# Two gated layers with a routed expert stage: expert outputs stored in blocks and gathered per token, 28 experts' weights kept

## The reference, cut to what matters

```
x = x + tanh(g_xattn[0]) * _L0_xattn_ref(ctx_512, _layernorm(x, axis=-1), ...)
x = x + tanh(g_ffn[0]) * _L0_ffn_ref(_layernorm(x, axis=-1), ...)
x = x + tanh(g_xattn[1]) * _L1_xattn_ref(...)
x = x + tanh(g_ffn[1]) * _L1_ffn_ref(_layernorm(x, axis=-1), ...)

def _L1_ffn_ref(hidden_states, gate_w, w_gate, w_up, w_down):
    probs = jax.nn.softmax(router_logits.astype(jnp.float32), axis=-1)
    top_vals, top_idx = jax.lax.top_k(probs, TOP_K)          # 8 of 64 experts for each of the 1024 tokens
    top_vals = top_vals / jnp.sum(top_vals, axis=-1, keepdims=True)
    rw = rw.at[jnp.arange(T)[:, None], top_idx].set(top_vals)
    g = jnp.einsum('th,ehi->tei', x, w_gate)                 # 256 -> 96
    u = jnp.einsum('th,ehi->tei', x, w_up)
    h = jax.nn.silu(g) * u
    h = h * rw[:, :, None]
    out = jnp.einsum('tei,eih->th', h, w_down)               # 96 -> 256
```

## Time and profile before

| | us |
|---|---|
| median of 3 runs | 408.3 |
| lowest and highest | 407.87, 409.57 |
| the profiled execution, its own time | 411.4 |
| its span, first to last instruction | 409.7 |
| PE busy in the span | 289.1 (71%) |
| DVE busy | 231.8 (57%) |
| POOL busy | 212.3 (52%) |
| ACT busy | 138.5 (34%) |
| moved by DMA | 98.39 MB, 240 GB/s over the span |

### The profile page before, as it was taken

How to read it: one execution, slowest core, us unless ns; L and a number is a source line. 1 busy time by engine, 2 the same in 40 slices (tenths; PEclk the granted TensorE clock), 3 DMA queues, 4 the chain that set the end, 5 groups by cost and what they waited for, 6 DMA issues and landing times.

```text
span 409.7 us, 7438 instructions
## 1 busy us (share of the span) xinstructions
PE 289.1 (71%) x2042; PEld 234.1 (57%) x2042; DVE 231.8 (57%) x1114; ACT 138.5 (34%) x393; POOL 212.3 (52%) x257
## 2 busy tenths in 40 slices
PE   5898168127810610899876778989899977871997
PEld 1345057126810510788765666878788855541886
DVE  0799999989397472355632433565655533331352
ACT  2263354315634420244432233444444432320000
POOL 2632013013358777777777777777777774540000
PEclk9999999657975555799999899999999999975899
DMA  4899997270016633999999999749999999726991
GB/s 134 306 341 300 302 322 226 80 228 3 1 48 224 232 128 131 316 330 324 324 331 311 338 326 318 234 136 297 301 326 300 305 289 267 214 58 251 346 299 62
DMA packets 72983, 98.39 MB, mean 240 GB/s; under 512 B 13007, under 2 KB 66144, under 8 KB 71920
## 3 DMA queue, kind: packets, MB, share of 16 engines
q1 hardware_dynamic: 63728, 79.03, 63.0%
q0 software_dynamic: 9216, 18.90, 14.5%
HBM read 62.23 MB, written 39.85 MB: 249 GB/s over the span
## 4 chain that ended last, share of the span: by engine, by line
PE 44%; DVE 22%; DMA 14%; POOL 9%; issue 5%; SPq 3%; ACT 3%; DVEq 0%; POOLq 0%; ACTq 0%
PE psum L756 16%; PE psum L765 10%; POOL expert_rows L514 8%; PE psum L812 7%; DVE work L1036 5%; DMA token_picks<-down_w,target 5%; DVE top L1032 5%; PE psum L745 4%; DMA gu_w<-expert_rows 3%; DMA sim<-expert_rows 3%; DVE xn L1154 2%; DVE stats L1007 2%; PE psum L576 2%; PE psum L570 2%; DMA sim<-token_picks 1%
## 5 line engine op out<-in xcount | busy, mean ns | idle before, releaser
L765 PE MATMUL psum<-proj_t,gu_w 96*96 96x256 f32 x254 | 77.5, 387 | 5.0 <-DVE gu_w L1247 5.0
L514 POOL DMA_INDIRECT expert_rows<-x_rows,place_at x64 | 62.5, 977 | 23.8 <-issue 22.9
L534 POOL DMA_INDIRECT token_picks<-down_w,target x64 | 58.7, 917 | 25.1 <-issue 14.4
L534 POOL DMA_INDIRECT token_picks<-adj,target x63 | 57.8, 917 | 22.5 <-issue 13.7
L967 ACT ACTIVATE gu_w<-psum 96x96 f32<-96x96 f32 x127 | 31.3, 246 | 108.2 <-PE psum L756 107.7
L1247 DVE TENSOR_TENSOR gu_w<-gu_w,psum 96x96 f32<-96x96 f32 x127 | 31.6, 249 | 56.8 <-ACT gu_w L967 56.0
L756 PE MATMUL psum<-gu_w,wgu 128*96 128x96 f32 x504 | 56.0, 256 | 7.7 <-DVE gu_w L1242 7.6
L756 PEld LDWEIGHTS psum<-gu_w,wgu 128*96 128x96 f32 x504 | 49.8, 170 | 9.6 <-DVE gu_w L1242 9.3
L1242 DVE COPY gu_w<-psum 128x192 f32<-128x192 f32 x127 | 43.7, 344 | 0.0
L745 PEld LDWEIGHTS psum<-ident,gu_w 96*128 96x128 f32 x160 | 22.0, 145 | 30.0 <-issue 12.3
L745 PE MATMUL psum<-ident,gu_w 96*128 96x96 f32 x160 | 27.7, 256 | 15.0 <-DMA gu_w<-expert_rows 14.4
(11 more groups left out here) (182 smaller groups left out, 448.2 us busy)
## 6 DMA issues: line engine op xcount, KB each, us to landing
expert_rows<-empty_rows SPq DMA_DIRECT2D x1, 15360.0 KB, 69.8
wgu<-in_L_ffn_w_gate_up SPq DMA_DIRECT2D x57, 192.0 KB
proj_t<-in_L_ffn_w_down SPq DMA_DIRECT2D x113, 96.0 KB
gu_w<-expert_rows SPq DMA_DIRECT2D x80, 120.0 KB
base<-in_L_ffn_w_gate_up SPq DMA_DIRECT2D x35, 192.0 KB
sim<-expert_rows SPq DMA_DIRECT2D x48, 120.0 KB, 2.0
pen<-in_L_ffn_w_gate_up SPq DMA_DIRECT2D x21, 192.0 KB
gu_w<-in_L_ffn_gate_up_proj SPq DMA_DIRECT2D x4, 512.0 KB, 8.1
```

Source lines behind the costliest of these rows:

```text
L514: pool.indirect_dma_start(rows_dram, bass.IndirectOffsetOnAxis(ap=place_at[:, t, k:k + 1], axis=0), x_rows[:, t, :], None).then_inc(placed ...
L534: pool.indirect_dma_start(picks_dram, bass.IndirectOffsetOnAxis(ap=target[0:SLOTS, n, i:i + 1], axis=0), y_slots[n][0:SLOTS, i, :], None, ...
L765: last = pe.matmul(psum[0:SLOTS, 4 + e % 2, i * D:(i + 1) * D], h1_t[:, e % 2, i * SLOTS:(i + 1) * SLOTS], wd[:, n, :], start=True, stop=True)
```

## The change

`expert_rows` keeps only the 256 numbers of a token (1 KB rows). A unit's 96 result rows are no longer scattered by POOL: ACT issues one plain DMA, which stores them as a block in a new DRAM buffer `y_rows`, two units later (`store_rows`). POOL gathers them per token when they are all there: one indirect DMA for each tile and pick, 64 in all (`gather`), the 32 of the first half once the first half's blocks are stored, the 32 of the second half once all blocks are. DVE sums the 8 picks (`sum_pick`, scalar_tensor_tensor on 128x256, one after the other); the sums of the first half stand between units of the second half, three in four units. The diagonal matrices and their multiplications on PE are gone. DVE works out the positions and the picked weights in 128 small steps (`pick_step`, four to a unit from unit 4 on).

Gate, up and down weights of an expert lie in one array of 128 x 640 numbers, in which the down part is padded from 96 to 128 partitions, so that one DMA of 320 KB loads them. There are 28 slots for them, in tiles that are free by then. Units run experts 63 to 1 on the first half, then the overflow loop (one turn here: expert 0 of the first half), then experts 1 to 63 and 0 on the second half. All of the first 63 units load (28 of them ahead of the stage), and 36 of the last 64. Rows and results have 8 slots each. POOL issues all placings ahead of anything else in the stage. SP also clears 86 blocks of `y_rows` (8.3 MB more to write early, against 3.1 MB less for the narrower `expert_rows`).

```diff
-CAP = SLOTS * SUBS
-W_RING = 16
-W_OWN = 8
-X_RING = 16
-Y_RING = 16
-T_RING = Y_RING
-K_RING = 4
+CAP = SLOTS
+W_OWN = 4
+X_RING = 8
+Y_RING = 8
...
+    units = [(e, e) for e in range(NE - 1, 0, -1)] + [(NE + e, e) for e in range(1, NE)] + [(NE, 0)]
+    UNITS = len(units)
+    FIRST = NE - 1
+    MAX_OVER = T * TOP_K_EXPERTS // CAP + 2
+    Y_ROWS = (UNITS + MAX_OVER) * CAP
...
+    rows_dram = nc.dram_tensor("expert_rows", [NR * REGION, D], F32, kind="Internal").ap()
+    y_dram = nc.dram_tensor("y_rows", [Y_ROWS, D], F32, kind="Internal").ap()
+
+    y_units = y_dram.rearrange("(u n) d -> u n d", n=CAP)
...
+        w_own = sb("w_own", [P, W_OWN * W])
+        w_slots = []
+        for home, n in ((w_own[:], W_OWN), (flat(proj_rows), 6), (flat(base), 3), (flat(pen), 3), (flat(gu_w), 6), (flat(down_w), 3), (flat(y0_t), 3)):
+            w_slots += [home[:, i * W:(i + 1) * W] for i in range(n)]
+        W_RING = len(w_slots)
...
+        x_slots = [flat(sim)[:, n * D:(n + 1) * D] for n in range(X_RING)]
+        y_slots = [flat(work)[:, n * D:(n + 1) * D] for n in range(Y_RING)]
...
+        picks = [flat(adj), flat(x_rows), flat(adj), flat(x_rows), flat(sim), flat(work), flat(adj), flat(x_rows)]
...
+        for u, (region, e) in enumerate(units):
+            n = (NE - 1 - e) % W_RING
+            if resident.get(n) != e:
+                seen[n] += 1
+                resident[n] = e
+                w_load_of[u] = True
+                w_before[u] = last_user.get(n, -1) + 1
+            last_user[n] = u
+            w_count[u] = 16 * seen[n]
...
+                if u + X_RING == FIRST:
                     for b in (2, 3):
                         sp.wait_ge(placed[b], 16 * HB * TOP_K_EXPERTS)
                 if u + X_RING < UNITS:
                     load_rows(u + X_RING)
...
-            picks_f = picks_dram.rearrange("(t p k) d -> t p (k d)", p=P, k=TOP_K_EXPERTS)
-            for t in range(NT):
-                need(sp, picks_summed, t - K_RING + 1)
-                sp.dma_start(picks[t % K_RING], picks_f[t]).then_inc(picks_landed[t % K_RING], 16)
+                for later in range(max(u, W_RING), UNITS):
+                    if w_before.get(later) == u - 1:
+                        load_weights(later)
...
+            for t in range(PER):
+                need(pool, picks_summed, (t - 1) * TOP_K_EXPERTS)
+                gather(t)
+            for n in range(Y_RING):
+                pool.wait_ge(y_stored[n], y_stored_by(n, UNITS))
+            for t in range(PER, NT):
+                need(pool, picks_summed, (t - 3) * TOP_K_EXPERTS if t >= PER + 2 else 0)
+                gather(t)
...
+            def store_rows(u):
+                n = u % Y_RING
+                act.wait_ge(y_ready, u + 1)
+                act.dma_start(y_units[u if u < FIRST else u + MAX_OVER], y_slots[n][0:CAP]).then_inc(y_stored[n], 16)
...
+            for u in range(UNITS):
+                silu_gate(u)
+                if u >= 2:
+                    store_rows(u - 2)
+                if u:
+                    copy_y(u - 1)
+                if u == FIRST - 1:
+                    over_units()
+            store_rows(UNITS - 2)
             copy_y(UNITS - 1)
-
...
+            def pick_step(n):
+
+                what, t, k = n // (NT * TOP_K_EXPERTS), n // TOP_K_EXPERTS % NT, n % TOP_K_EXPERTS
+                values, picks_of = ((rank, y_pick), (rw, pick_w))[what]
+                dve.scalar_tensor_tensor(out=picked[:, n % 32], in0=order[:, t], scalar=float(TOP_K_EXPERTS - k), in1=values[:, t],
+                                         op0=ALU.is_equal, op1=ALU.mult, accum_out=picks_of[:, t, k:k + 1]).then_inc(pick_ready, 1)
...
+            def sum_pick(t, k):
+                if k == 0:
+                    dve.wait_ge(picks_landed[t], 16 * TOP_K_EXPERTS)
+                    dve.wait_ge(x3_ready, t + 1)
+                else:
+                    dve.wait_ge(picks_summed, t * TOP_K_EXPERTS + k)
+                last = dve.scalar_tensor_tensor(out=xs[:, t], in0=picks[t][:, k * D:(k + 1) * D], scalar=pick_w[:, t, k:k + 1], in1=xs[:, t] if k else x3[:, t],
+                                                op0=ALU.mult, op1=ALU.add).then_inc(picks_summed, 1)
+                if k == TOP_K_EXPERTS - 1:
+                    dve.wait_ge(picks_summed, (t + 1) * TOP_K_EXPERTS)
+                    dve.sem_inc(out_ready, 1)
...
+            for u in range(UNITS):
+                up_times_silu1(u)
+                if u + 2 < UNITS:
+                    copy_slots_t(u + 2)
+                if u == FIRST - 1:
+                    over_units()
...
+                if u == FIRST:
+                    dve.wait_ge(pick_ready, 2 * NT * TOP_K_EXPERTS)
+                while n_summed < min((u - FIRST - 18) * 3 // 4, PER * TOP_K_EXPERTS):
+                    sum_pick(n_summed // TOP_K_EXPERTS, n_summed % TOP_K_EXPERTS)
+                    n_summed += 1
+            for n in range(n_summed, NT * TOP_K_EXPERTS):
+                sum_pick(n // TOP_K_EXPERTS, n % TOP_K_EXPERTS)
...
+    down = _np.asarray(inputs["L1_ffn_w_down"])
+    down = _np.pad(down, ((0, 0), (0, P - down.shape[1]), (0, 0)))
+    w_expert = _np.ascontiguousarray(_np.concatenate([gate_up, down], axis=2))
```

More of the change, by code:

```diff
@@ L538, in _ @@
-            for u in range(UNITS):
-                if u % 3 < 2 and late:
-                    b, n = late.pop(0)
-                    place_rows(b, n, n + 1)
-                scatter(u)
-            total_over = load_over(pool)
-            with pool.Fori(0, total_over) as j:
-                pool.wait_ge(y_ready, j + (UNITS + 1))
-                pool.wait_ge(over_target_ready, j + 1)
-                pool.sem_inc(over_begun, 1)
-                for i in range(SUBS):
-                    pool.indirect_dma_start(picks_dram, bass.IndirectOffsetOnAxis(ap=over_target[0:SLOTS, i:i + 1], axis=0),
-                                            y_slots[LAST_Y][0:SLOTS, i, :], None, bounds_check=T * TOP_K_EXPERTS - 1, oob_is_err=False).then_inc(scattered[LAST_Y], 16)
+            place_rows(2, 0, PICKS)
@@ L749, in gate_up1, with transpose_slots @@
-            def gate_up1(e):
-                n = units[e][1] % W_RING
-                pe.wait_ge(xt_copied, e + 1)
-                pe.wait_ge(w_landed[n], w_count[e])
-                need(pe, h_ready, e - 1)
+            def transpose_slots(u):
+                pe.wait_ge(x_landed[u % X_RING], 16 * (u // X_RING + 1))
+                need(pe, xt_copied, u - 1)
+                for k in range(KC):
+                    last = pe.transpose(psum[:, u % 2, k * CAP:(k + 1) * CAP], x_slots[u % X_RING][0:CAP, k * P:(k + 1) * P], ident[0:CAP, 0:CAP])
+                last.then_inc(xt_filled, 1)
@@ L754, in gate_up1 @@
+            def gate_up1(u):
+                n = (NE - 1 - units[u][1]) % W_RING
+                pe.wait_ge(xt_copied, u + 1)
+                pe.wait_ge(w_landed[n], w_count[u])
+                need(pe, h_ready, u - 1)
                 for part in range(2):
                     for k in range(KC):
-                        last = pe.matmul(psum[0:I1, 2 + e % 2, part * CAP:(part + 1) * CAP], wgu[n][:, k, part * I1:(part + 1) * I1],
-                                         x_slots_t[:, e % 2, k, :], start=k == 0, stop=k == KC - 1)
+                        last = pe.matmul(psum[0:I1, 2 + u % 2, part * CAP:(part + 1) * CAP], gate_up_of(w_slots[n])[:, k, part * I1:(part + 1) * I1],
+                                         x_slots_t[:, u % 2, k, :], start=k == 0, stop=k == KC - 1)
@@ new lines, in _ @@
+            for n in range(PHASES):
+                some = slice(n * PER, (n + 1) * PER)
+                last = dve.scalar_tensor_tensor(out=y_extra[:, some], in0=rank[:, some], scalar=float(CAP), in1=per_token(y_shift[:, n]), op0=ALU.is_ge, op1=ALU.mult)
+            link(last)
+            for n in range(PHASES):
+                some = slice(n * PER, (n + 1) * PER)
+                last = dve.tensor_tensor(rank[:, some], rank[:, some], per_token(y_first[:, n]), ALU.add)
+            link(last)
```

463 lines of the change are left out of this document (197 added, 266 removed).

## The result

| | before | changed |
|---|---|---|
| median, us | 408.77 (407.87 to 409.57, 4 runs) | 415.09 (414.01 to 416.4, 4 runs) |
| ratio | | 1.0161, 95% interval 1.0123 to 1.0199 |
| the profiled execution, own time | 411.4 | 414.29 |
| its span | 409.7 | 412.5 |

The change makes the kernel 6.3 us slower; forecast were 418.3, range 402 to 430.

A forecast was written before the change was run, and what follows sets the result against it. DMA was taken to bound the loading stretches, PE's 1.28 us the other units, POOL's issuing the end. Units to 367.9 plus a 51.8 us tail gave 419.7, 10.0 above the span; against the median 418.3 us, range 402 to 430.

The forecast's parts named there:

- unit 44 there: End of the first half's loading stretch: 22.1 MB at 329 GB/s take 67.2 us, to 237.2.
- unit 64: End of the first half: 20 more PE periods at 1.28 us, 25.6 us, to 262.8, with DMA little used.
- overflow: Its turn, moved between the halves, where all engines stand for it: 5.5 us.
- unit 107: End of the second half's loading stretch: 22.8 MB at 329 GB/s take 69.3 us, to 340.2.
- tail: After the last down: store, 32 POOL gathers at 1.26 us (40.3 us), landing, sums, output; 51.8 us, 4.9 more than before.
- the 329 of the mix before: Loading stretches: DMA rate kept at the old 329 GB/s despite 2.5 KB rows, since half the bytes are in 1 KB rows.
- Subtracting 3.1 at the end: Last step of the sum: the profiled execution lay 3.1 us above the median, so the forecast became 418.3 us.
- The mark I set for myself: Loading stretches: 44.9 MB must take under 126.5 us, 355 GB/s on average, for the kernel not to be slower.
- rival 3: ACT's queue becomes the bound if an issue exceeds 0.67 us: 15 us, 433; chance 0.16 shared with a 307 GB/s case.
- the 1.19 of 1.28: DVE in the units: four pick steps plus its two other instructions take 1.19 of 1.28 us, costing nothing.
- Rival 1: Loading stretches: larger rows lift the DMA limit; at 391 GB/s 21.7 us less, 396.6 us; chance 0.20.
- Rival 2: No change: a rate of 353 to 361 GB/s, or a gather at 0.96 us, brings 406 to 410; chance 0.08.

The follow-up runs named there:

- the second profile: Changed kernel and kernel before, both unaltered, profiled again one after the other on one chip: 414.31 us and 409.19 us.
- the split load: Changed kernel with each weight load issued as two DMAs (rows of 1.5 and 1 KB), same bytes: 419.78 us, ratio 1.0288 to the kernel before.
- the spread kernel: Changed kernel with the weight loads in SP's queue issued in two of three units instead of one per unit: 396.77 us, ratio 0.9738 to the kernel before.

## Why the prediction was right, point by point

*Direction and size.* Slower, as forecast; 415.09 against 418.3, or 6.3 us more than before where 10.0 were forecast. The terms against both profiles of the changed kernel (rates over the whole transfer):

| step | forecast | first profile | second |
|---|---|---|---|
| start of the stage | 166 | 165.0 | 165.5 |
| unit 44 there, rate | 237.2 at 329 GB/s | 232.6 at 364 | 235.9 at 350 |
| unit 64 | 262.8 | 258.2 | 261.5 |
| overflow | 5.5 | 7.0 | 5.9 |
| unit 107, rate | 340.2 at 329 GB/s | 331.6 at 348 | 333.3 at 356 |
| unit 126 | 364.5 | 356.3 | 357.6 |
| last down ends | 367.9 | 359.7 | 361.1 |
| tail | 51.8 | 52.8 | 52.7 |
| span | 419.7 | 412.5 | 413.8 |

*The mis-sized term* is "I take the 329 of the mix before". The two transfers took 62.6 and 63.8 us, 126.4 together (170 to 232.6 and 267.8 to 331.6), at 356 GB/s on average, and 128.5 at 353 in the second profile, where I had 136.5. Half the bytes being in 1 KB rows did not hold the rate down as I argued; the split load shows that the other half's rows matter, but only for part of it. The second transfer's bytes also had a load too many, the 36th, which is issued at 350.11: 1 us at 329 GB/s.

*Luck.* Against the execution it was reckoned from, the sum said 10.0 us more, and that pair shows 2.8: the transfers came out 10.1 shorter, and 2.9 of that went again at the overflow (1.5), the tail (1.0) and the second half's last units (0.4). That the medians are 6.3 apart, nearer to the 10.0, comes mostly from an execution of before that lay high, not from the sum. Subtracting 3.1 at the end brought the forecast nearer too (it would have been 421.4), but no term of the sum held that surplus, which lay at the end of the second half of before (278 GB/s against 296 in its second profile).

*The mark I set for myself was off.* "355 or more proves me wrong", and 126.5 us as the point from which the kernel isn't slower. Rate and time came out on that mark in the first profile (356 GB/s, 126.4 us) and near it in the second (353, 128.5), and the kernel was slower all the same. Two things were missing from the mark. It was worked out against the high execution; against the span of 405.8 the point is some 4 us lower, near 366 GB/s. And it took all other terms at their forecast, where they came to 2.9 us more (2.2 in the second profile).

*Right:* clearing cost nothing (the changed kernel's first unit transposes at 164.99, before at 164.91); PE's period stayed 1.28 us with ACT's issue, DVE's steps and sums beside it, so rival 3 did not occur, an issue on ACT taking 0.32 and not above 0.67 (the units from 174 to 183 us ran at 1.28 with four pick steps each, where I had counted on over 1.5; the 1.19 of 1.28 held); loads front-loaded, then 20 units with DMA half idle; the tail's gathers, 1.27 us each on average against 1.26. What the tail has above the forecast lies behind them: 3.5 us from the last sum (ends 408.97) to the end of the span, where I had 2.2.

*The overflow* cost 7.0 us in the first profile (10.87 from unit 64 to 67, less three periods of 3.84 together) and 5.9 in the second, against 5.5. It stops a PE that runs at speed on either side: behind it eight gate and up multiplications took 1.49 us twice where they take 0.84, with the granted clock at 6 tenths in that slice (1.49 and 1.34 in the second profile). In the spread kernel the page has the clock at 9 there, and from unit 64 to 68 it took 9.9 us against 12.2.

*Rival 1* (transfers faster, 396.6 us) had the right direction of the rate and not its size: 356 and 353, not 391. *Rival 2* named a rate of 353 to 361 and 406 to 410 us: the rate came, the time didn't, for the two reasons above.

*The rule of the skill.* The Trainium skill, "DMA: Bandwidth & Descriptors", Specifications: about 358 GB/s of HBM to a core, line rate from 512 B on. The mean of the transfers, 356 and 353, comes near that figure, but for this one core alone no limit stands there: the first stretch ran at 368 and 370 over 52 us in two profiles, slices of 10 us at up to 399. And the split load lost 22 GB/s in the first stretch though all its rows stayed above 512 B, which disagrees with the second half of the rule if it was the rows; their number of DMAs changed with them. Using the page's figure would have brought the transfers closer (125.4 us against the 126.4 and 128.5 measured).

## What to carry to other kernels

Bytes saved are worth only what the queue's order lets them be: a load issued as soon as its slot is free bunches all loads in front and leaves the engines idle behind, and here spacing them turned 6 us lost into 12 us won. When work is moved off one engine's issuing into another phase, count its instructions where nothing covers them: 32 gathers at 1.25 us are 40 us of the tail, with the DMA engines at a share of 0.37 beside them. And work out a decision point against a typical execution, not against the one that happened to be profiled; two executions of the same changed kernel already had unit 44 3.3 us apart.

## What the runs showed of the hardware that I had not expected

Removing scatters and merging loads raised the rate from 334 and 311 to 368 and 357 GB/s while the DMA share stayed at 1.03 to 1.06: a full share doesn't fix the bytes.

A gather of 128 rows takes POOL 1.25 us (0.95 busy, 0.30 between two), as a placing of 128 rows does (0.96 and 0.30), and a plain DMA takes ACT 0.32 us to issue. Where PE waits for a 96 KB row load in the two transfers, the chain of waits of the first profile has it landing 11.0 to 13.3 us after its issue, behind 320 KB weight loads in the same queue; ahead of the stage one landed in 2.1 us.
